# Full attention that stores its outputs by dimension, and an output stage without transposes

## The reference, cut to what matters

```
q = x' wq^T, k = x' wk_a^T wk_b^T, v = x' wv_a^T wv_b^T       16 heads of 16 columns, rotary on q and k
scores = q k^T / 4 ;  attn = softmax(scores) over all 1024 keys ;  out = attn v
x1 = x + gate * (out wo^T)                                    gate: one row of 256 per batch entry
h  = (layernorm(x1)) * scale + shift                          input of the next stage, stored in two halves
```

## Time and profile before

| | |
|---|---|
| time, median of 3 runs | 4847.93 us (4840.43 to 4849.11) |
| the profiled execution | 4837.09 us, its span 4835.1 us |
| mean granted TensorE clock | 0.949 of full speed |
| PE busy | 4276.8 us, 88% of the span |
| DVE busy | 3590.9 us, 74% |
| ACT busy | 2801.1 us, 58% |
| POOL busy | 1616.5 us, 33% |
| DMA | 297.05 MB, mean 61 GB/s |

### The profile page before, as it was taken

The page is one execution under the profiler, slowest core; times in us unless marked ns, Lnnn a source line. Parts: engine busy times, 40 slices in busy tenths (PEclk is TensorE's granted clock), DMA queues, the critical chain, the costliest instruction groups (busy, mean ns, idle before and its releaser), DMA issues. The chain is left out here.

```text
span 4835.1 us, 94881 instructions
## 1 busy us (share of the span) xinstructions
PE 4276.8 (88%) x27610; PEld 2744.2 (57%) x27610; DVE 3590.9 (74%) x7998; ACT 2801.1 (58%) x6209; POOL 1616.5 (33%) x2408
## 2 busy tenths in 40 slices
PE   5869999999999976599999997999799999988998
PEld 2423333333333334477777775888577777766787
DVE  6579888888888949688888784454688888875554
ACT  2438777777777850366666663333566666653333
POOL 2300000000000004455555553433455555545545
PEclk8969999999999998799999997999999999998999
DMA  6933323233233317200000002111100000012221
GB/s 204 367 54 61 60 42 60 46 57 54 48 61 50 52 63 243 72 25 26 24 24 26 24 23 63 44 54 35 49 24 25 25 24 25 25 30 85 68 65 51
DMA packets 368130, 297.05 MB, mean 61 GB/s; under 512 B 65820, under 2 KB 324888, under 8 KB 367648
## 3 DMA queue, kind: packets, MB, share of 16 engines
q1 hardware_dynamic: 367648, 291.11, 24.5%
HBM read 178.74 MB, written 111.21 MB: 60 GB/s over the span
## 5 line engine op out<-in xcount | busy, mean ns | idle before, releaser
L889 ACT ACTIVATE fa_P<-fa_pS 128x512 f32<-128x512 f32 x2048 | 1112.0, 595 | 385.7 <-PE fa_pS L815 337.6
L916 DVE TENSOR_REDUCE fa_mx<-fa_pR 128x2 f32<-128x1024 f32 x1024 | 1205.4, 1221 | 151.3 <-PE fa_pR L796 139.5
L1518 POOL TENSOR_TENSOR wa_pn<-wa_pr,wa_ri 128x512 f32<-128x512 f32 x512 | 700.7, 1369 | 614.0 <-DVE wa_ri L1574 600.4
L815 PE MATMUL fa_pS<-fa_Q,fa_K 50*128 50x512 f32 x2048 | 520.2, 504 | 108.0 <-ACT fa_P L889 77.8
L1454 ACT ACTIVATE wa_pr<-wa_sm,wa_mn 128x256 f32<-128x256 f32 x1024 | 510.4, 501 | 177.5 <-DVE wa_mn L1566 177.5
L1140 POOL TENSOR_TENSOR ao_xn<-ao_xn,ao_mod 128x1024 f32<-128x1024 f32 x16 | 37.6, 2348 | 1663.5 <-DVE ao_xn L1105 1663.5
L830 PE MATMUL fa_pO<-fa_P,fa_V 128*32 128x512 f32 x4096 | 560.1, 620 | 0.2 <-ACT fa_P L889 0.2
L815 PEld LDWEIGHTS fa_pS<-fa_Q,fa_K 50*128 50x128 f32 x2048 | 194.6, 187 | 602.9 <-ACT fa_P L889 543.4
L796 PE MATMUL fa_pR<-fa_K,fa_Q 48*128 48x512 f32 x2048 | 406.8, 451 | 60.6 <-DMA fa_K<-parts_d 38.5
L1306 PE MATMUL wa_pQK<-wa_wqkv,wa_xT 128*128 128x512 f32 x1536 | 419.7, 409 | 5.8 <-DVE wa_qa L1611 5.8
L2012 ACT ACTIVATE ff_gl<-ff_pG,ff_b 128x512 f32<-128x512 f32 x192 | 132.6, 691 | 475.2 <-PE ff_pG L1953 475.2
(11 more groups left out here) (186 smaller groups left out, 7191.8 us busy)
## 6 DMA issues: line engine op xcount, KB each, us to landing
parts_d<-pj_parts SPq DMA_DIRECT2D x64, 512.0 KB, 5.4
fa_Q<-parts_d SPq DMA_DIRECT2D x192, 128.0 KB, 4.5
fa_K<-parts_d SPq DMA_DIRECT2D x192, 128.0 KB, 6.9
v_d<-pj_v SPq DMA_DIRECT2D x16, 1024.0 KB, 8.4
fa_V<-v_d SPq DMA_DIRECT2D x32, 512.0 KB, 8.8
pj_x<-in_L_attn_x SPq DMA_DIRECT2D x16, 512.0 KB, 7.6
fa_Q<-fa_nrow SPq DMA_DIRECT2D x512, 2.0 KB
att_d<-fa_att SPq DMA_DIRECT2D x64, 128.0 KB, 2.0
```

The costliest lines, as they stand in the source:

```text
L815: nc.tensor.matmul(pS[:, (s * exped.per + u + e) % T, :], Ks[at:at + SROWS + 2, s, a, kb * P:(kb + 1) * P], Qs[at:at + SROWS + 2, s, a, ha ...
L889: nc.scalar.activation(Pr[:, k % 2, h, :], pS[:, (s * exped.per + u) % T, :], ACT.Exp).then_inc(exped.sem, 1)
L916: nc.vector.tensor_reduce(mx[:, q // QB, :, a, q % QB, kh], row_slot(), AX.X, ALU.max).then_inc(row_free, 1)
L1518: nc.gpsimd.tensor_tensor(pn[:, hp % 2], pr[:, hp % 2], inv, ALU.mult).then_inc(s["weighted"].sem, 1)
```

## The change

In full attention:
- `OT` (16 rows of outputs and one of sums per head) is stored as it is: four DMAs of 16 rows x 512 to `num_d` (by dimension) and one of the four rows of sums to `den_d`. The transposes and `divide` go. The sums of a whole group are loaded back as 128 x 32, inverted by VectorE in step 6 of the next group, and stored to `inv_d`.
- The maxima keep their sign (`Ks` holds -1 in place of 1). Pool splits them into high and low parts before the transpose; TensorE turns 16 columns of both together in a score slot, in steps 2 and 10; ScalarE copies them out. The counters `scored` and `exped` now count slots, 66 per group.
- The first maxima are turned after all 32 row scores of the first group, in place of after 16.
- SyncE's order in a group becomes load, store, wait for the stores, row DMAs, sums.

In the output stage Pool multiplies the stored outputs by the inverse sums (loaded with each head's row repeated over 16 partitions) and, once per batch entry, the weights `wo` by the gate row; TensorE multiplies with these; VectorE only adds x. The two PSUM tiles `pY` alternate.

```diff
 # SyncE, a group of full attention
+    rows_ = num_d.rearrange("(g c) b t -> g c b t", g=NG)[bass.ds(g, 1), :, bass.ds(b, 1), cols]
+    sp.wait_ge(o_out.sem, o_out.upto(n, half + 1))
+    for h in range(GH):
+        dst = rows_[:, h * HD:(h + 1) * HD].rearrange("g c b t -> (g c) (b t)")
+        sp.dma_start(dst, OT[h * 32:h * 32 + HD, half, :]).then_inc(stored[half].sem, 16)
+    dst = den_d[bass.ds(b, 1), bass.ds(g * GH, GH), cols]
+    sp.dma_start(dst.rearrange("b h t -> (b h) t"), OT[HD:P:32, half, :]).then_inc(stored[half].sem, 16)
...
     def body(n, s):
-        max_rows(n, s, 1)
         if not (isinstance(n, int) and n + 2 >= GROUPS):
             load(n + 2, (s + 2) % NB)
         if not is_first(n):
             store(n - 1, 1)
+            sums_stored(n - 1)
+        max_rows(n, s, 1)
+        if not is_first(n):
+            load_sums(n - 1)
+            store_inverse(n - 1)
+        store(n, 0)
         if not is_last(n):
             max_rows(n + 1, (s + 1) % NB, 0)
-        store(n, 0)
...
 # TensorE
+    def turn_max(n, half):
+        pe.wait_ge(top_steps.sem, top_steps.upto(n, 3 * half + 3))
+        if not (is_first(n) and half == 0):
+            pe.wait_ge(exped, turn_tile(n, half) - T + 1)
+        nc.tensor.transpose(pS[0:2 * MCOLS, turn_slot(n, half), 0:P],
+                            tops[:, half].rearrange("p x c -> p (x c)").bitcast(F32), ident[:]).then_inc(scored, 1)
     def scores(n, s, k, a):
-        if not (is_first(n) and u < 2):
-            pe.wait_ge(exped.sem, n * exped.per + u - 1)
+        if not (is_first(n) and k == 0 and a == 0):
+            pe.wait_ge(exped, tile(n, k, 2 * a + 1) - T + 1)
...
 # ScalarE, behind the exponentials of steps 2 and 10
+    def max_out(n, s, half):
+        act.wait_ge(scored, turn_tile(n, half) + 1)
+        nc.scalar.copy(trow[:, s, half, :], pS[0:2 * MCOLS, turn_slot(n, half), 0:P]).then_inc(exped, 1)
...
 # VectorE, in group n
+    def invert(n):
+        dve.wait_ge(den_in.sem, den_in.upto(n))
+        nc.vector.reciprocal(inv[:], den[:]).then_inc(inverted.sem, 1)
...
             if not is_last(n):
-                row_max(2 * k)
-                row_max(2 * k + 1)
+                row_max(n + 1, 2 * k)
+                row_max(n + 1, 2 * k + 1)
+            if k == KB - 2 and not is_first(n):
+                invert(n - 1)
...
 # output stage, Pool
+    def divide(n, r):
+        pool.wait_ge(loaded.sems[r], loaded.upto(n))
+        if later(n):
+            pool.wait_ge(projected.sem, projected.upto(n - 2))
+        if r % 2 == 0:
+            row = mrow[:, r, 0, :].unsqueeze(1).to_broadcast([P, KT, D])
+            nc.gpsimd.tensor_tensor(wg[:, r // 2], w["wo"][:], row, ALU.mult).then_inc(aT_ready.sem, 1)
+        nc.gpsimd.tensor_tensor(aT[:, r % 2], nT[:, r], iT[:, r], ALU.mult).then_inc(aT_ready.sem, 2 - (r + 1) % 2)
...
+    def body(n, r, following=True):
+        if following:
+            divide(n + 1, (r + 1) % R)
+        modulate(n, r)
...
 # output stage, VectorE
     def body(n, r, following=True):
         stats_of(n, r, range(0, 6))
         if following:
-            gate(n + 1, (r + 1) % R)
-        stats_of(n, r, range(6, 8))
-        if following:
             add(n + 1, (r + 1) % R)
-        stats_of(n, r, range(8, LN_INCS))
+        stats_of(n, r, range(6, LN_INCS))
         normalize(n, r)
```

More of the change, by code:

```diff
@@ new lines, in store, with sums_of, sums_stored @@
+                    sp.dma_start(dst.rearrange("b h t -> (b h) t"),
+                                 OT[HD:P:32, half, :]).then_inc(stored[half].sem, 16)
+                def sums_of(x, n):
+                    b, g = n // NG, n % NG
+                    one = x[bass.ds(b, 1), bass.ds(g * GH, GH), :]
+                    return one.rearrange("b h (c t) -> (b h c) t", c=DEN_C)
+                def sums_stored(n):
+                    for half in range(2):
+                        sp.wait_ge(stored[half].sem, stored[half].upto(n))
@@ L834, in turn_sums @@
[L834 to L842, removed]
+                                         start=True, stop=True).then_inc(scored, 1)
@@ new lines, in sums @@
+                def sums(n, s, k, part):
+                    kb, at = k % KB, part * (HALF // PV_PARTS)
+                    if part == 0:
+                        pe.wait_ge(exped, tile(n, k, GH - 1) + 1)
+                        if k == 0:
+                            pe.wait_ge(v_in.sems[s], v_in.upto(n))
+                            if not is_first(n):
+                                pe.wait_ge(o_out.sem, o_out.upto(n - 1))
+                        if k == KB:
+                            pe.wait_ge(o_out.sem, o_out.upto(n, 1))
+                    cols = slice(at, at + HALF // PV_PARTS)
+                    for h in range(GH):
+                        last = nc.tensor.matmul(pO[h * 32:(h + 1) * 32, cols], V[:, s, kb, h, :], Pr[:, k % 2, h, cols],
+                                                start=(kb == 0 and part == 0),
+                                                stop=(kb == KB - 1 and part == PV_PARTS - 1))
+                    if part == PV_PARTS - 1:
+                        last.then_inc(summed.sem, 1)
@@ L843, in _ @@
+                for j in range(ROWS):
                     row_scores(0, 0, j)
                 turn_max(0, 0)
-                for j in range(ROWS // 2, ROWS):
-                    row_scores(0, 0, j)
                 def body(n, s):
-                    use[0], use[1] = first_use(n), 0
                     for k in range(STEPS):
[L851 to L855, removed]
+                        before = None
@@ L872, in _ @@
-                turn_sums(GROUPS - 1, 1)
+                for part in range(PV_PARTS):
+                    sums(GROUPS - 1, (GROUPS - 1) % NB, STEPS - 1, part)
             @block.scalar
@@ L1067, in body, with add @@
                     last.then_inc(projected.sem, 1)
                 drive(pe, body)
[L1071 to L1079 removed]
             @block.vector
             def _(dve):
[L1083 removed]
+                def add(n, r):
```

366 lines of the change are left out of this document (164 added, 202 removed).

## The result

The changed kernel takes 5,030.9 us (median of 4 runs, 5,022.9 to 5,065.3), the kernel before 4,848.5 in the same session (4,840.4 to 4,865.0): the ratio is 1.038, 95% interval 1.033 to 1.043. The forecast was 5,125 with a range of 4,945 to 5,180. The median lies in the range, but under the 5,060 to 5,180 that the forecast gave for its main case.

A forecast was written before the change was run, and what follows sets the result against it. Full attention was taken as a ring with no engine full, the output stage as paced by VectorE. 4,837.1 - 37.8 + 17.3 + 6.8 + 6 + 93 + 72 + 125 = 5,119; median 5,125 us, range 4,945 to 5,180.

The forecast's parts named there:

- main case: Whole kernel: forecast as summed, with stalls and clock loss in full attention; own range 5,060 to 5,180 us, chance 0.58.
- SyncE's order, the step called dearest: Full attention: stores behind 2 MB of loads land late, VectorE waits for the sums, TensorE stands; +93 and +72 us.
- T: Full attention: time 0 at a group's first exponential; loads forecast at -1.1, the sums landing at 22.7 us.
- Its count and its price: Full attention, groups 1 to 29: 29 stalls, each 3.2 us of delay and 2.5 us of slow clock.
- The Trainium skill's smaller bill: Full attention: stores land in about 2 us, sums in time, no stall; 165 us less, 4,960; chance 0.15.
- The ring: Full attention's step cycle of TensorE and ScalarE: output transposes gone, -37.8 us; maxima's turn in a score slot, +17.3 us.
- The turned maxima's step: Full attention, steps 2 and 10: transposing maxima in a score slot makes the step 2.96 us, +0.27.
- The start: Before the first scores: a copy, eight DMA issues (4.93) and a landing now stand ahead; +6.8 us.
- The output stage: Output chunks: Pool's products lengthen the period from 9.6 to 17.9 us mean; 15 x 8.3 = +125 us.
- The circle: Output stage: Pool modulates and divides, TensorE projects, VectorE adds, finishes its chain and normalizes, nothing overlapping; 17.5 and 18.9 us.
- The faster rival: Output stage: VectorE stays the bound, Pool's product and the projection hide beside its chain; 4,817 us; chance 0.04.

The follow-up runs named there:

- loads-last kernel: Changed kernel with SyncE issuing the loads for the group after next behind the load of the row sums: 4,910.2 us, ratio 1.013.
- Pool ahead in both: Pool divides two output chunks ahead, before the modulation: on the changed kernel (loads first) 4,944.6 us; with SyncE's loads last as well 4,820.9 us.
- the kernel with both orders right: Changed kernel with SyncE's loads behind the load of the row sums and Pool dividing two chunks ahead: 4,820.9 us, ratio 0.995.
- the filled last group: Both order edits plus VectorE making the product; last attention group's row scores and maxima made once more and thrown away: 4,820.9 us, ratio 0.9949.

## Why the prediction was right, and where its sizes were off

- **SyncE's order, the step called dearest: right.** Loads first, SyncE past its wait for the stores behind them at T + 15.5 (15.2 was forecast), reciprocal at T + 23.3 (22.7), TensorE standing in step 8, the clock down behind it in all 21 groups with a stall. That the loads ahead cause it, and not the number of stores, is shown by the loads-last kernel: no stall, and attention 154.3 us shorter, 4.9 of which is its shorter last group. Moving VectorE's question by a step either way moves the time in the forecast direction: a step later takes nearly all the slow clock away, a step sooner adds standing alone.
- **Its count and its price: both off, in opposite directions.** The forecast had 29 stalls of 3.2 + 2.5 us, 165 in all. The trace has 21: in the 8 groups right behind a turn of the loop, T comes late by the turn's gap, the loads start at T - 4 and the sums are in time. The 21 cost more each. The bill: attention's +128.6, plus the ring's gain of 29, less 22 for the slow last group, leaves 136 us, 6.5 for each; against the loads-last kernel it is 149 us, 7.1 each. These are bills of the longest execution. With Pool ahead in both, loads first and loads last differ by 128 us over groups 1 to 30, and the medians differ by 121 and 124 us: some 6 for each of the 21. So the forecast's 165 was too dear as a whole, against 121 to 149 by pair. How it divides can be estimated: a slow step loses 1.45 of its 4.14 us, 35%. Outside the last group attention had 297 us of slow clock against 75 before; 35% of the 222 more is 78 us, 3.7 a stall; some 2.8 are left for the standing itself. So by this estimate the wait was forecast well (3.2) and the clock too small (2.5, bounds 0 to 4.5). No run took the clock away and left the standing; the one with the reciprocal sooner lengthened the standing alone.
- **The Trainium skill's smaller bill**, "DMA: Bandwidth & Descriptors", section "Latency and other measured facts", with about 2 us for a DMA: it holds with nothing ahead (at most 2.5 us from last issue to the wait passed, loads last) and doesn't behind 2 MB of loads (6.3). The forecast that followed from it, 4,960, is what didn't happen.
- **The ring: direction right, gain too small.** A half is 21.76 us where 21.90 was forecast and 22.22 was before. The turned maxima's step is 2.94 (707.87 to 710.81; forecast 2.96), the copy 0.26 (0.3). What I left in the sum was the 0.13 by which the step with the output copy was late: that is 0.02 now (754.29 to 757.00 with the copy between). 64 x 0.46 = 29 us against 20.5.
- **The start: wrong in sign.** The wait before the first scores came as priced (6.55 us at 305.89, for rows whose DMAs stand behind the copy), but the first scores still start 1.4 us sooner than in the earlier trace rows. The failed step: "now the copy and eight DMA issues (4.93) and a landing stand before them" left out that the first loads now wait for one filled buffer instead of all, and are issued at 249.21 instead of 256.10. The first group's row scores end 8.5 us sooner.
- **The output stage: mechanism right, size 18% over.** The circle is as written, Pool then TensorE then VectorE with nothing beside it. A chunk takes 17.2 us (17.9 forecast), and the chunk before took 10.1, not 9.6. That 9.6 was read from the row, whose last start, 1948.3, is where that view's window ended and not the last normalization (1955.3, start of the last chunk's four). Two small errors of one sign, 15 x (0.7 + 0.5) = 18 us. The faster rival, in which VectorE stays the bound, was rightly put low; the kernel with both orders right comes near it, at 11.2.
- **What the forecast didn't have.** The last group ran at half clock for the 61.4 us of the window above, some 22 us in this profile. Without it attention would have been +107 against the forecast +144.5, so that the two stand as near each other as they do is in part luck. In the rest of the program, whose code nobody touched, it was 12.5 us quicker; over ten profiles of nine kernels that part takes 2,840 to 2,871 us (from the first transposes of window attention on), and both profiles of the kernel before lie at the upper end, as does the one with the filled last group. I can't say why. The 34 us between the profiled execution and the median aren't explained by it: that execution's 2,854 is only 15 us above the lowest. Its stalls may have cost more than usual (see the bills above) and its last group is the slowest of all profiles; which of them it was isn't shown.
- **Still open.** Whether the missing row scores make the clock fall in the last group. The filled kernel kept full clock there, and the seven other profiles of the changed kernel and its variants all have some 10 us or more of slow clock in it; but the filled one is one profile only, and the kernel before did the same in one of its two without any filling. Open too is what sets the 11 us of a chunk with both orders right.

## What to carry to other kernels

A store whose arrival something waits for must not be issued behind bulk loads on the same queue; with 2 MB ahead of it the wait was 6.3 us instead of at most 2.5, and moving the loads two lines down took 2.5% off the kernel. When an operation is moved to another engine, write down the circle it joins: with Pool's product one chunk ahead it hid nowhere and a chunk took 17.2 us, two ahead 11.1 to 11.2, against 10.1 before. And when a wait leaves TensorE standing for 2.7 us, price the slow clock behind it as well, here by the estimate above at more than the wait itself (3.7 against 2.8 us). It didn't grow with the wait: stalls 2.3 us longer brought no more slow clock.

## What the runs showed of the hardware

- A step at the 1.2 GHz level takes 4.14 us where it takes 2.69 at 2.4 GHz. TensorE stood 2.73 us right before the 13.7 us stretch shown, and 2.3 to 2.8 us at each of the eight loop turns of the kernel before, where the clock fell every time (for 10.2 us in the earlier trace rows; 3.4 to 13.7 in the others).
- Some of VectorE's small operations are held while Pool runs a large one. One 128x4 operation (L84) takes 0.16 us alone and 2.3 when it starts beside Pool's 1024-column product, ending 0.03 us after it (1852.52 and 1852.48 above). The statistics of the layer norm (L365, 0.41) and its aggregates (L370, 0.15) take the same beside Pool's product as alone. The large additions aren't held either: 1.22 us beside Pool too, but there Pool's gated weights took 2.16 us instead of 1.26 (1844.70, same kernel). So a Pool product moved off the critical path can still be on it through VectorE.
